# A selective scan and a routed feed-forward on one core: drives in place in PSUM, one-state units, gathers and mixes moved behind the last routing

## The reference, cut to what matters

```
# layer 1: a selective scan with 16 states a channel
xn    = layernorm(layernorm(x)) * gamma + beta
dt    = softplus(xn @ W_dt.T + b_dt);  A = -exp(A_log)
B, C  = xn @ W_B.T, xn @ W_C.T                       # 16 values a token
h[t]  = exp(dt[t] * A) * h[t-1] + dt[t] * B[t] * xn[t]      # per channel and state
y[t]  = sum over the states of C[t] * h[t] + D_param * residual
x     = x + layernorm(y)
# layer 2: 8 experts, the 2 best for each token
u     = layernorm(x);  p = softmax(u @ gate_w + gate_b);  top 2 of p
out   = sum over the 2 of p * (relu(u @ w1[e] + b1[e]) @ w2[e] + b2[e])
x     = x + layernorm(out)
```

## Time and profile before

| | before |
|---|---|
| median of 3 runs | 640.55 us |
| the profiled execution's own time | 640.66 us |
| its span, first to last instruction | 638.9 us |
| TensorE's mean granted clock | 0.794 of full |
| instructions | 8953 |
| last scan ends | 447.1 us |
| last routing ends | 498.1 us |
| last tile's output made | 600.5 us |

### The profile page before, as it was taken

How to read it: one execution, slowest core, us unless ns; L and a number is a source line. 1 busy time by engine, 2 the same in 40 slices (tenths; PEclk the granted TensorE clock), 3 DMA queues, 4 the chain that set the end, 5 groups by cost and what they waited for, 6 DMA issues and landing times. The chain is left out here.

```text
span 638.9 us, 8953 instructions
## 1 busy us (share of the span) xinstructions
PE 430.5 (67%) x2548; PEld 347.2 (54%) x2548; DVE 395.3 (62%) x693; ACT 325.4 (51%) x854; POOL 377.3 (59%) x229
## 2 busy tenths in 40 slices
PE   1466676753747795979796977988569626399610
PEld 0144444532535675868585766867558615389510
DVE  1499998988748789897888976789226100220022
ACT  3573662552336585666786635755248312286311
POOL 1368468356997834887878867779811637210171
PEclk9995675566558999798898959789979867599955
DMA  2873233433405675464497516544435525277111
GB/s 59 304 262 124 84 133 115 128 134 99 170 25 187 206 210 191 143 192 131 115 384 201 208 50 202 173 131 113 121 92 141 157 61 159 50 178 174 38 51 41
DMA packets 69599, 91.64 MB, mean 143 GB/s; under 512 B 6696, under 2 KB 50480, under 8 KB 65456
## 3 DMA queue, kind: packets, MB, share of 16 engines
q1 hardware_dynamic: 60848, 49.11, 27.6%
q10 hardware_dynamic: 4608, 33.56, 14.0%
q0 software_dynamic: 4096, 8.40, 4.4%
HBM read 72.43 MB, written 18.61 MB: 142 GB/s over the span
## 5 line engine op out<-in xcount | busy, mean ns | idle before, releaser
L533 POOL TENSOR_TENSOR ch<-hs,c_rep 128x1024 f32<-128x1024 f32 x64 | 174.4, 2734 | 63.2 <-DVE hs L791 62.7
L791 DVE TENSOR_TENSOR_SCAN hs<-ab,bx 128x1024 f32<-128x1024 f32 x64 | 187.7, 2942 | 7.8 <-ACT ab L664 4.7
L712 ACT ACTIVATE hid_t<-hid_ps,w_tile 128x128 f32<-128x128 f32 x368 | 104.1, 371 | 83.6 <-PE hid_ps L1101 38.4
L1113 PE MATMUL out_ps<-w_f,hid_t 128*128 x736 | 110.4, 298 | 25.2 <-ACT ot L720 22.0
L1026 PE MATMUL y_ps<-ident,ch 128*128 128x128 f32 x512 | 91.9, 339 | 44.8 <-POOL ch L533 44.5
L1113 PEld LDWEIGHTS out_ps<-w_f,hid_t 128*128 128x128 f32 x736 | 98.4, 208 | 34.8 <-issue 33.8
L1026 PEld LDWEIGHTS y_ps<-ident,ch 128*128 128x128 f32 x512 | 76.3, 177 | 63.5 <-POOL ch L533 56.1
L664 ACT ACTIVATE ab<-dt,decay 128x512 f32<-128x512 f32 (+1 forms) x128 | 85.1, 717 | 49.2 <-DVE hs L791 38.2
L1101 PE MATMUL hid_ps<-xt_t,w_tile 128*128 128x128 f32 x736 | 104.3, 291 | 5.4 <-ACT hid_t L712 2.4
L553 POOL DMA_INDIRECT yg<-slots_out,pos x64 | 71.2, 1113 | 62.1 <-DMA slots_out<-ot 44.4
L543 POOL DMA_INDIRECT slots_in<-x,pos x64 | 85.8, 1340 | 33.2 <-DVE expert L907 16.6
(11 more groups left out here) (123 smaller groups left out, 415.9 us busy)
## 6 DMA issues: line engine op xcount, KB each, us to landing
c_rep<-c_dram ACTq DMA_DIRECT2D x32, 1024.0 KB, 7.1
w_tile<-w_rows SPq DMA_DIRECT2D x92, 258.0 KB
slots_in<-zeros SPq DMA_DIRECT2D x4, 1472.0 KB, 8.3
slots_out<-ot SPq DMA_DIRECT2D x44, 128.0 KB
xt<-slots_in SPq DMA_DIRECT2D x20, 256.0 KB
xs<-x SPq DMA_DIRECT2D x8, 256.0 KB, 3.0
out<-mix SPq DMA_DIRECT2D x8, 256.0 KB, 2.8
slots_in<-x,pos POOLq DMA_INDIRECT x64
```

The source lines that it names most:

```text
L533: nc.gpsimd.tensor_tensor(ch[:, n % NCH], hs[:, n % NH], c_rep[:, r // 2, 2 * (r % 2):2 * (r % 2) + 2].rearrange("p n t -> p (n t)"), ALU. ...
L712: last = nc.scalar.activation(hid_t[:, q % 2, c * P:(c + 1) * P], hid_pair[q % 2][:, c * P:(c + 1) * P], ACT.Relu, bias=w_tile[:, q % NW, ...
L791: nc.vector.tensor_tensor_scan(hs[:, n % NH], ab[:, n % 2], bx[:, n % 2], 0.0, ALU.mult, ALU.add).then_inc(s["scanned"], 1)
L1113: last = nc.tensor.matmul(out_ps[:, j * D:(j + 1) * D], hid_t[:, q % 2, c * P:(c + 1) * P], w2_f[:, bass.ds(e * HC * D + c * D, D)], start ...
```

## The change

It rewrites the pair's work as two units of one state; unit i is state h of pair n, i = 2n + h.

- `b_ps` becomes three single banks, used in turn. `drive` writes its product in place into the bank, and `scan` reads `ab` from SBUF and that bank from PSUM. Both have 512 elements. `bx` is gone; `ab` has five buffers of 512.
- `rep` of unit i waits for scan i-3, `decay` of unit i for scan i-5. Product and reduce stay as they were, one for a pair.
- The bank `turn` is gone: `tile_turn` writes into `misc`, by the rule of `misc_free`.
- `hid_t` has three buffers. From the tile `alone` on (the first that the plan starts after the last scan) the hidden values rotate over five banks, the three of `b_ps` and the two of their own.
- In the plan, gathers wait for the last scan, and `bias_mix` and `mix` for the last routing (`slots` of the last group). Prices for drive, scan and rep are new. `order` runs the plan twice to find `alone`, then once with it.

```diff
-    "stats": 1.8, "shift_x": 0.25, "rest": 0.7, "drive": 1.25, "scan": 2.7, ...
+    "stats": 1.8, "shift_x": 0.25, "rest": 0.7, "drive": 0.66, "scan": 1.22, ...
...
-            at(1, "rep", n, 0, ("rest", b, 0), ("drive", n - 1, 0))
-            at(3, "drive", n, 0, ("rep", n, 0), ("dt_gx", b, 0), ("scan", n - 2, 0))
             for h in range(2):
-                at(1, "decay", n, h, ("dt_gx", b, 0), ("scan", n - 2, 0))
-            at(4, "scan", n, 0, ("drive", n, 0), ("decay", n, 1), ("weigh", n - NH, 0))
-            at(1, "weigh", n, 0, ("scan", n, 0), ...)
+                at(1, "rep", n, h, ("rest", b, 0), ("scan", *before(n, h, NBX)))
+                at(3, "drive", n, h, ("rep", n, h), ("dt_gx", b, 0))
+                at(1, "decay", n, h, ("dt_gx", b, 0), ("scan", *before(n, h, NA)))
+                at(4, "scan", n, h, ("drive", n, h), ("decay", n, h), ("weigh", n - NH, 0))
+            at(1, "weigh", n, 0, ("scan", n, 1), ...)
...
-            at(6, "tile_up", q, 0, ..., ("tile_relu", q - 2, 0), ("tile_up", q - 1, 0))
-            at(4, "tile_relu", q, 0, ("tile_up", q, 0), ("tile_down", q - 2, 0))
+            at(6, "tile_up", q, 0, ..., ("tile_up", q - 1, 0),
+               *((("tile_relu", q - NBX - NHID, 0), scan_of(END - 1)) if q >= alone else (("tile_relu", q - NHID, 0),)))
+            at(4, "tile_relu", q, 0, ("tile_up", q, 0), ("tile_down", q - NHT, 0))
...
-                at(3, "gather", b, r, ("mix", b - 2, 0),
+                at(3, "gather", b, r, ("mix", b - 2, 0), scan_of(END - 1),
...
-            at(4, "bias_mix", b, 0, ("weigh_copy", b, 0), ("store", b - NMIX, 0), *(("gather", b, r) for r in range(TOPK * K)))
-            at(2, "mix", b, 0, ("bias_mix", b, 0))
+            at(4, "bias_mix", b, 0, ("weigh_copy", b, 0), ("store", b - NMIX, 0), ("slots", len(GROUPS) - 1, 0),
+               *(("gather", b, r) for r in range(TOPK * K)))
+            at(2, "mix", b, 0, ("bias_mix", b, 0), ("slots", len(GROUPS) - 1, 0))
...
-        b_ps = bank("b_ps", 2)
+        b_ps = [bank(f"b_ps{i}") for i in range(NBX)]
-        turn = bank("turn")
-        hid_pair = [bank("hid_ps0"), bank("hid_ps1")]
+        hid_ps = [bank(f"hid_ps{i}") for i in range(NHID)]
...
+        def hidden(q):
+            if q < alone:
+                return hid_ps[q % NHID]
+            free = b_ps + [hid_ps[(alone + i) % NHID] for i in range(NHID)]
+            return free[(q - alone) % len(free)]
...
-                nc.vector.tensor_tensor(bx[:, n % 2]..., b_ps[:]..., gx[:, b % 2, None, :].to_broadcast([P, 2, T]), ALU.mult)
+                nc.vector.tensor_tensor(b_ps[i % NBX][:], b_ps[i % NBX][:], gx[:, b % 2], ALU.mult).then_inc(s["driven"], 1)
...
-                nc.vector.tensor_tensor_scan(hs[:, n % NH], ab[:, n % 2], bx[:, n % 2], 0.0, ALU.mult, ...)
+                if h == 0:
+                    after(dve, s["weighed"], n - NH + 1)
+                nc.vector.tensor_tensor_scan(hs[:, n % NH, h * T:(h + 1) * T], ab[:, i % NA], b_ps[i % NBX][:], 0.0, ALU.mult, ...)
...
-                after(pe, s["driven"], n)
-                for h in range(2):
-                    last = nc.tensor.matmul(b_ps[:, h * T:(h + 1) * T], choose[...].to_broadcast([64, P]), ...)
+                after(pe, s["scanned"], i - NBX + 1)
+                nc.tensor.matmul(b_ps[i % NBX][:], choose[...].to_broadcast([64, P]), ...).then_inc(s["b_rep"], 1)
...
-                after(pe, s["tile_ready"], m)
+                misc_free("tile_turn")
...
-                after(pe, s["hid_t_ready"], q - 1)
+                if q >= alone:
+                    pe.wait_ge(s["scanned"], 2 * END)
+                after(pe, s["hid_t_ready"], q - (NBX + NHID if q >= alone else NHID) + 1)
```

More of the change, by code:

```diff
@@ L57 @@
 NCH = 2
+NA = 5
+NBX = 3
+NHID = 2
+NHT = 3
 OUTS = 2
@@ L109, in scan_of, with before @@
     def scan_of(n):
-        return ("scan", n, 0)
+        return ("scan", n, 1)
+    def before(n, h, far):
+        return (2 * n + h - far) // 2, (2 * n + h - far) % 2
     at(0, "weights_2", 0, 0, scan_of(0))
@@ L201, with planned @@
 MISC_USE = {"turn": "channels", "states": "rest", "delta": "softplus", "turn_u": "skip_copy", "gate_turn": "gate_copy",
-            "gate_logits": "gate_bias", "count": "starts", "weigh_turn": "weigh_copy", "bias_mix": "mix"}
+            "gate_logits": "gate_bias", "count": "starts", "weigh_turn": "weigh_copy", "bias_mix": "mix", "tile_turn": "tile_copy"}
 def order():
-    todo = tasks()
+    alone = ALL_TILES
+    for _ in range(2):
+        steps = planned(alone)
+        last = max(time for time, kind, i, _ in steps if kind == "scan") + COST["scan"]
+        alone = 1 + max(i for time, kind, i, _ in steps if kind == "tile_up" and time < last)
+    return planned(alone), alone
+def planned(alone):
+    todo = tasks(alone)
     left = {key: len(set(after)) for key, (_, after) in todo.items()}
@@ L412, in program @@
         zeroed = [ctx.enter_context(nc.semaphore(f"zeroed{g}")) for g in range(len(GROUPS))]
-        steps = order()
+        steps, alone = order()
         def after(eng, sem, n):
@@ L522, in dt_gx @@
                 pool.wait_ge(s["dt_ready"], b + 1)
[L523 removed]
+                after(pool, s["driven"], N * (b - 1))
                 nc.gpsimd.tensor_tensor(gx[:, b % 2], dt[:, b % 2], xa[:, b % 2], ALU.mult).then_inc(s["gx_ready"], 1)
@@ L943, in _ @@
             shift_x(0, 0)
-            for i in range(2):
-                nc.vector.memset(ab[:, i, T:T + 1], 0.0)
             for r in restart.values():
@@ L1075, in tile_turn @@
                 pe.wait_ge(tile_loaded[m % NB], 16 * (m // NB + 1))
-                after(pe, s["tile_ready"], m)
+                misc_free("tile_turn")
                 for j in range(n):
-                    last = nc.tensor.matmul(turn[:, j * P:(j + 1) * P], xt[:, m % NB, j], ident[:], start=True, stop=True,
+                    last = nc.tensor.matmul(misc[:, j * P:(j + 1) * P], xt[:, m % NB, j], ident[:], start=True, stop=True,
                                             is_transpose=True)
```

75 lines of the change are left out of this document (35 added, 40 removed).

## The result

The changed kernel takes **614.79 us** (median of 4 runs, 612.84 to 618.79) against 638.67 (4 runs, 636.7 to 642.35): ratio 0.963, 95% interval 0.955 to 0.970. Faster, but by 24 us where 76 were forecast, and outside the range. The profiled execution took 616.42 us, its span is 614.7.

A forecast was written before the change was run, and what follows sets the result against it. VectorE, 84% full in the scan stage, was taken as the bound there, its scans locked against GpSimd's products. Terms -51, -18 and -7 give -76 on 640.66 us: 565 us, forecast 545 to 585, range 532 to 612.

The forecast's parts named there:

- The lock: Scan stage: a scan with both inputs in SBUF waits for GpSimd's product; one input in PSUM ends this, 31.5 us less.
- Scan stage, -51: Up to the last scan: 422 us become 371, VectorE's work 326 and idle 45; 51 less (30 to 76).
- Last scan to last routing, -18: Without mixes and gathers in the chain, 51 us become 33; 18 less (0 to 21).
- The 30 us worked out from the earlier trace for the chain itself: Last scan to last routing: product and reduce 3.3 us, 13.2 to the logits, 13.1 to the end.
- Scatters, loads and tiles, -7: After the last routing: scatters and first loads unchanged at 32 us; last group's tiles 71 to 64, 7 less.
- half a stop of 14 us: Last group's tiles: half of the earlier ScalarE relu wait beside GpSimd's gathers stays, giving 64 us.
- The end, unchanged: Last gathers, mixes and stores after the last tile: 38 us, unchanged.
- The condition stated in the sum: After the last scan, GpSimd's 87 us of moved work is hidden if gathers 2 to 5 start before the tiles end.
- C: Drives: in-place work on one PSUM bank runs at half rate, scan stage gets 68 us back: 633 us; chance 0.05.
- D: Drives and scans both slower from PSUM, 136 us in all: 701 us; chance 0.05 with milder forms from 647 up.
- E: Scan stage: the lock stays, a pair still takes 4.6 us: 608 us; chance 0.05.
- A: Scan-stage idle stays 66.6 us, tile stops double, half the routing gain is lost: 621 us, halfway 593; chance 0.17.

The follow-up runs named there:

- run 3: The changed kernel, but the drive writes its product to SBUF and the scan reads both inputs from SBUF: 669.21 us, ratio 1.049.
- run 5: The changed kernel, but in the plan the gathers follow the last group's last scatter instead of the last scan: 615.4 us.
- run 15: The changed kernel with a 256-element GpSimd addition as a pause ahead of each gather of sequences 0 to 4: 579.50 us, ratio 0.905.
- Run 18: The changed kernel with a 128-element GpSimd addition ahead of each gather of sequences 0 to 4: 557.84 us, ratio 0.923; the kernel before took 604.1 us with it.
- run 2: The kernel before with only the plan's new conditions for gathers, bias_mix and mix; scans keep both inputs in SBUF: 649.77 us, ratio 1.016.
- run 8: The changed kernel, but the plan keeps every add of GpSimd behind the last group's scatters: 620.7 us.
- run 7: The changed kernel with weigh_turn at urgency 3 instead of 7 and bias_mix at 3 instead of 4: 617.4 us.
- run 11: The changed kernel with a 512-element addition ahead of each gather of sequences 0 to 5, and weigh_turn and bias_mix at urgency 3: 601.95 us, ratio 0.939.
- runs 6, 10, 13 and 15: The changed kernel with 512-element additions ahead of gathers of sequences 0 to 5 (599.2 us), those plus last-group scatters (605.53), sequences 0 to 4 (594.96); run 15 above.
- run 16: The changed kernel with gathers behind the last group's scatters and those of sequences 0 to 3 spaced by additions: 591.78 us, ratio 0.921.
- runs 17 and 18: Run 17: the changed kernel with a 256-element addition ahead of gathers of sequences 0 to 4 and the last group's 16 scatters: 572.63 us, ratio 0.946. Run 18 above.
- runs 9 to 12: Kernel before with paced gathers (640.55 us); changed kernel with paced gathers and scatters (605.53), paced gathers and earlier weigh_turn (601.95), paced gathers and order undone (624.51).

## Why the prediction was wrong

**The lock, right.** Removed with all its prices, as run 3 confirms.

**Scan stage, -51: mis-sized, -68.** The forecast's 326 us of work and 45 of idle were 300 and 55 (299.77 of 354.50). Of the 26 us of work, 8 lie in scans and drives (150.1 and 84.8 us for 156 and 87), the others in short instructions whose stretch the forecast left in: over the whole run, all of VectorE's instructions but scans and drives take 111.6 us for 130.2.

**Last scan to last routing, -18: the first step that failed.** It was +2. The forecast named the burst and allowed 3 us for it; it costs 19 (52.7 against run 5's 33.7). The 30 us worked out from the earlier trace rows for the chain itself are 4 short.

**Scatters, loads and tiles, -7: failed most.** Forecast 96 us from routing to last tile, measured 128.3. The step that failed is the price of the stops. The forecast kept half a stop of 14 us among the tiles and took the scatters as unchanged; but with the new order dense gathers and scatters follow each other from the last scan on, and TensorE's signals are held beside both. Spacing the gathers takes away 18 of the 32 us too many (run 15, 110.3 us); signals held up to 11.6 us beside its dense scatters are left in it. Run 18, without any late signal, has the same 36 and 51 tiles done at its last scan and routing and needs 94.2 us from there to the last tile, 2 less than forecast:

```profile
409.20:503.40 94.20, 87.98 (x704) 82.53 (x704) 12.15 (x54) 62.28 (x211) 52.13 (x67) 0.98 0.67 186
```

That the held signals are worth all of the 32 us is thus likely, but not shown: run 18 has pauses, ran where the kernel before took 604.1 us, and no trace of that kernel was kept from there.

The forecast also added up stages as if each had its own work. TensorE's tiles run under the scans; now 14 fewer are done at the last scan (36 for 50) and 12 fewer at the last routing. TensorE is busy 88 us behind it (run 18) where it was busy 68 of 102 before: the tiles that moved fill idle time from which a shorter stage could have come. Their number is the plan's and not the chip's. Every run with the plan of the PSUM part has 36 at its last scan, run 3 too, where that scan comes at 432.4 us; run 2, at 430.1, has 46. Whether more would fit under the shorter scans wasn't tried. The add's wait of 12 us, which the forecast didn't foresee, costs little by itself (run 8).

**The end, unchanged: failed, +16.** The forecast put four more mixes among the tiles. One more is there (three for two), and three more stand behind them: VectorE's 90 instructions of the last window are five mixes of 18, for 36, two mixes, in the earlier trace rows. The condition stated in the sum (gathers 2 to 5 start before the tiles end) failed for sequence 5: its gathers wait for mix 3, `weigh_turn(3)` has urgency 7, and while tiles are left it stands behind them. This, too, is the plan's doing: the end takes 54 us in run 3, with slow scans, and in runs 15 and 18, with and without late signals. Undoing it isn't free: three mixes more among the tiles lengthen them by 18.8 us in run 7 and 21.8 in run 11, 6 to 7 us each.

**Rivals.** C, D and E are excluded by 1204 and 688 ns. A's time was near (593 to 621), but that is luck: VectorE's idle fell from 66.6 to 55 us, and the stops that A doubles among the last group's tiles aren't there (58.2 us for 68.2); they lie ahead of them, beside the gathers and scatters. By stages the span changed by -68 to the last scan, +2 to the last routing, +26 to the last tile (102.4 and 128.3 us) and +16 to the end: -24. Against the forecast that is -16.5, +19.7, +32.3 and +16.1 us, which are the 52 between the forecast's 564.7 and the profiled 616.42.

## What to carry to other kernels

When a stage gets shorter, count what other engines did beneath it, and move that work behind it in the sum: a stage-by-stage sum takes free cover for granted. Where the kernel's own plan fixes the order, count in the plan: tiles done at the last scan and mixes behind the last tile could be read from it before any run (playing `order` of the two kernels gives 49 and 36 tiles, two and five mixes). A wait "remote" beside indirect DMAs of GpSimd is a price of their density; a pause of 0.6 us ahead of each, where matmuls run beside them, returned 35 us here (614.8 to 579.5; 0.905 of the kernel before for 0.963). Where the effect is absent a pause has nothing to give back; the kernel without pauses wasn't run there. Judge a reordering only once such a stop is out of the way: the same one was worth 0 and then 15 us.

## What the runs showed of the hardware

- **TensorE's signals wait beside dense indirect DMAs** (one each 1.25 us), up to 14 us in the two kernels and 20 in run 5; those of VectorE, ScalarE and GpSimd never, in 1351 waits of two traces. Beside DMAs spaced at 1.87 us or more (runs 6, 10, 13 and 15) none begins to wait, though ones held since a dense stretch came up to 6 us after its end (run 16: last scatter 434.1 us, signal 439.90). Whether the gap itself or what GpSimd does in it matters wasn't told apart.
- **It isn't always there**: beside runs 17 and 18 no signal was late, and the kernel before took 604.1 us, on the same chip on which it had taken 639.0 beside runs 9 to 12. So it isn't a matter of the chip alone; what else differed stays open. What the change itself brings there isn't known either, since the kernel after wasn't run there.
- **A VectorE instruction with both inputs in SBUF stands while GpSimd multiplies or adds there; with one in PSUM it doesn't.** Run 3 against the kernel after: scans of 1637 ns for 1204 in the mean, 54 us in all. It holds for short ones too: 1.71 us for 0.22 beside an addition (runs 13 and 15).
- **A scan from PSUM is not dearer.** The two kernels of one-state units, durations (least, median, most, ns), from PSUM and then from SBUF:

```profile
L816 DVE TENSOR_TENSOR_SCAN hs<-ab,b_ps x128: 1181/1208/1221, 27.4 to 378.3; 128x512 f32<-128x512 f32 x128
```

```profile
L817 DVE TENSOR_TENSOR_SCAN hs<-ab,bx x128: 1190/1214/3934, 27.4 to 429.1; 128x512 f32<-128x512 f32 x128
```

The fixed 65 ns estimated from the Trainium skill (VectorE: DVE Perf Modes, "The TRN2 errata") is not there; the median from PSUM is 6 ns less, and the most, 1221 for 3934, is the lock again.
